# State products in row halves, a fold by transposes, and a new order in phases 0 and 7 of a state-space and butterfly kernel

## What is computed

```python
xz = einsum('bld,ed->ble', layernorm(x), in_proj_w); x_inner, z = split(xz, 2, -1)
x_conv = silu(causal_depthwise_conv(x_inner, conv_w) + conv_b)
x_dbl = einsum('bld,ed->ble', x_conv, x_proj_w)            # 33 wide
delta, B, C = softplus(x_dbl[..., 0]), x_dbl[..., 1:17], x_dbl[..., 17:]
h = h * exp(delta * A) + x_t * delta * B ; y = h @ C        # a scan over tokens
x = x + einsum('bld,od->blo', (y + x_conv * D) * silu(z), out_proj_w)
h = butterfly(layernorm(x) @ W_exp + b_exp, up_weights)     # 10 stages
x = x + butterfly(gelu(h + up_bias), down_weights) @ W_con + b_con + down_bias
```

## Time and profile before

| | |
|---|---|
| median of 3 runs | 568.49 us (566.38 to 570.36) |
| the profiled execution | 569.59 us, of which span 567.9 us |
| TensorE (PE) busy | 528.9 us, 93% of the span |
| VectorE (DVE) busy | 409.6 us, 72% |
| ScalarE (ACT) busy | 306.1 us, 54% |
| GpSimd (POOL) busy | 109.5 us, 19% |
| mean granted TensorE clock | 0.966 of 2.4 GHz |

### The profile page before, as it was taken

The page is one execution under the profiler, slowest core; times in us unless marked ns, Lnnn a source line. Parts: engine busy times, 40 slices in busy tenths (PEclk is TensorE's granted clock), DMA queues, the critical chain, the costliest instruction groups (busy, mean ns, idle before and its releaser), DMA issues.

```text
span 567.9 us, 8152 instructions
## 1 busy us (share of the span) xinstructions
PE 528.9 (93%) x2996; PEld 430.3 (76%) x2996; DVE 409.6 (72%) x860; ACT 306.1 (54%) x526; POOL 109.5 (19%) x96
## 2 busy tenths in 40 slices
PE   3998899888999999999999999999999999699896
PEld 3766676776897779887888778877888788578886
DVE  4859999587983799468966799379946894575532
ACT  2876883865239622874268623962287417431342
POOL 4042100230201301050103120130105021411110
PEclk9986979799999999999999999999999999799999
DMA  8542311200012001210112001200021002100011
GB/s 244 97 27 3 80 35 38 76 2 2 23 52 74 4 2 48 66 39 2 37 41 74 0 9 68 71 8 1 5 73 38 0 2 74 41 1 0 6 34 37
DMA packets 42619, 21.75 MB, mean 38 GB/s; under 512 B 26419, under 2 KB 41011, under 8 KB 42580
## 3 DMA queue, kind: packets, MB, share of 16 engines
q1 hardware_dynamic: 39940, 17.57, 13.0%
q10 hardware_dynamic: 2640, 3.67, 2.3%
HBM read 16.78 MB, written 4.46 MB: 37 GB/s over the span
## 4 chain that ended last, share of the span: by engine, by line
PE 48%; DVE 20%; issue 12%; ACT 9%; SPq 6%; POOL 3%; DMA 0%; DVEq 0%; ACTq 0%; POOLq 0%
PE wide L711 12%; PE acc L844 9%; PE wide L833 7%; SPq L420 5%; PE wide L822 4%; DVE xc L1552 2%; DVE xc L1555 2%; POOL x1b_xn L598 2%; DVE state L1516 2%; DVE hid_low L1429 2%; PE wide L804 2%; PE small L731 2%; PE wide L811 2%; DVE xc L1412 2%; ACT L1054 2%
## 5 line engine op out<-in xcount | busy, mean ns | idle before, releaser
L1054 ACT ACTIVATE hid_f<-wide,bias_up 128x512 f32<-128x512 f32 x64 | 44.0, 687 | 162.0 <-PE wide L833 161.6
L1412 DVE SCALAR_TENSOR_TENSOR xc<-xi,taps,xc 128x512 f32<-128x512 f32 x96 | 87.0, 911 | 4.0 <-ACT xc L1085 1.7
L844 PE MATMUL acc<-w_down_high,hid_high 128*128 128x256 f32 x256 | 73.2, 286 | 5.6 <-DVE hid_low L1429 5.4
L844 PE MATMUL acc<-w_down_high,hid_low 128*128 128x256 f32 x256 | 71.9, 281 | 0.0
L844 PE MATMUL acc<-w_down_low,hid_high 128*128 128x256 f32 x256 | 71.9, 281 | 0.0
L1429 DVE TENSOR_TENSOR hid_low<-hid_f,hid_high 128x512 fp32r<-128x512 f32 x64 | 46.3, 725 | 29.8 <-ACT hid_high L1163 29.2
L833 PE MATMUL wide<-xnT_ln2T_high,w_up_high 128*128 128x512 f32 x128 | 55.4, 432 | 3.4 <-DVE xnT_ln2T_low L1423 1.8
L522 POOL TENSOR_TENSOR rstd<-var_eps,minus_half 128x4 f32<-128x4 f32 x16 | 19.1, 1192 | 202.8 <-DVE var_eps L1317 202.8
L711 PE MATMUL wide<-xnT_ln1T_high,w_in_high 128*128 128x512 f32 x128 | 56.5, 441 | 1.1 <-DVE xnT_ln1T_low L1423 1.0
L822 PE MATMUL wide<-w_out,xc 128*128 128x256 f32 x256 | 56.7, 379 | 0.3 <-DVE xc L1555 0.3
L844 PEld LDWEIGHTS acc<-w_down_high,hid_high 128*128 128x128 f32 x256 | 48.0, 188 | 11.2 <-issue 8.2
(11 more groups left out here) (185 smaller groups left out, 1054.6 us busy)
## 6 DMA issues: line engine op xcount, KB each, us to landing
x_res<-in_L_attn_x_dram SPq DMA_DIRECT2D x9, 512.0 KB, 3.5
c_near<-c_of_tokens SPq DMA_DIRECT2D x8, 512.0 KB
out_dram<-x1b_xn SPq DMA_DIRECT2D x8, 512.0 KB, 2.9
x_ln<-in_L_attn_x_dram SPq DMA_DIRECT2D x7, 512.0 KB, 3.6
xc<-in_L_attn_in_proj_w_dram ACTq DMA_DIRECT2D x2, 512.0 KB, 7.1
xc<-in_L_ffn_W_exp_dram ACTq DMA_DIRECT2D x1, 1024.0 KB, 10.8
x1b_xn<-in_L_ffn_W_con_dram ACTq DMA_DIRECT2D x1, 1024.0 KB, 14.5
raw_out<-n_L_attn_out_proj_w_dram ACTq DMA_DIRECT2D x1, 512.0 KB, 7.0
```

Source lines behind the costliest of these rows:

```text
L844: last = pe.matmul(acc[:, c, :], hid[h][:, j % HRING, c * P:(c + 1) * P], w_down[w][:, j, 0:DM], start=j == 0 and c % 2 == 0 and n == 0, s ...
L1054: ins = act.activation(out_ap, in_ap, how.pop("func"), **how)
L1412: ins = dve.scalar_tensor_tensor(xc[u % BATCH][:, e, :], xi[:, e, tap:tap + TILE], taps[:, e, tap:tap + 1], xc[u % BATCH][:, e, :], ALU.mu ...
```

## The change

1. `ssm_output` is split into two calls, one for each pair of channel blocks, with `up(p, 3)` and `down(p, 1)` between them. The state products use half the rows at a time: the states at the starts of groups 0 and 1 lie in rows 0 to 63 and serve tokens 0 to 255, those of groups 2 and 3 in rows 64 to 127 serve tokens 256 to 511. A bank now holds one half of the tokens of two channel blocks. `gates` follows: four operations of 256 columns and two of 512 for a pair.
2. `xd_tokens_first` transposes all 128 rows and VectorE adds the halves while it reads (`take_xd`); `fold` is gone.
3. VectorE: `convolve(v, 1)` moves ahead of `diagonal_times_c`, `low_hidden(p, 0)` and the low parts of w_down ahead of `assemble`.
4. ScalarE loads the gelu table behind `copy_first_state`.
5. GpSimd: `residual_with_bias(u - 1)` moves to the head of unit u and no longer waits for the gates of u; memsets at the start move ahead of a reciprocal root.
6. Phase 0: the order of input products, light products and low parts. `low_parts(2)` moves ahead of `first_residual(0)`.
7. Phase 7: `up(p, 0)` to `up(p, 2)` move ahead of `step_sums`.
8. `last_ffn`: the last two down products, the last add and the last store go in halves of 256 tokens.

```diff
@@ the bank orders
-    WIDE_ORDER += uses(("up", range(3)), of=phase - 1) + uses(("y", range(CB)), of=phase)
-    WIDE_ORDER += uses(("up", range(3, 5)), of=phase - 1) + uses(("out", range(2)), of=phase)
+    WIDE_ORDER += uses(("up", range(3)), of=phase - 1) + uses(("y", range(2)), of=phase)
+    WIDE_ORDER += uses(("up", [3]), of=phase - 1) + uses(("y", range(2, CB)), of=phase)
+    WIDE_ORDER += uses(("up", [4]), of=phase - 1) + uses(("out", range(2)), of=phase)
@@ SyncE
-            store(UNITS - 1)
+            sp.wait_ge(first_half_final, 1)
+            store(UNITS - 1, slice(0, GR // 2))
+            read(sp, UNITS - 1, "down", 0)
+            store(UNITS - 1, slice(GR // 2, GR))
@@ GpSimd
             for u in range(UNITS):
+                if u:
+                    residual_with_bias(u - 1)
                 weigh_gaps(u)
...
-                if u:
-                    wait(pool, gated, u, CB)
-                    residual_with_bias(u - 1)
                 rstd_of(u, 1, var2, rstd2)
@@ TensorE
-                    last = pe.matmul(bank[:, c * P:c * P + XD], xdT[:, c * P:(c + 1) * P], fold[:, :], start=True, stop=True)
+                    last = pe.transpose(bank[:, c * P:(c + 1) * P], xdT[:, c * P:(c + 1) * P], ident[:, :])
...
+            def ssm_output(u, pair):
+                banks = [tile_of("y", 2 * pair + h, u) for h in range(2)]
+                for h in range(2):
+                    free(pe, u, "y", 2 * pair + h)
...
+                for q in range(2):
+                    g = 2 * pair + q
+                    for c in range(GR):
+                        at = q * HALF_TILE + c % 2 * P
+                        pe.matmul(banks[c // 2][:, at:at + P], x_tok[:, c, g * P:(g + 1) * P],
+                                  m_mat[:, c * P:(c + 1) * P], start=q == 0 and c % 2 == 0, stop=False,
+                                  skip_group_check=True)
...
+                for q in range(2):
+                    g = 2 * pair + q
+                    for h in range(2):
+                        rows = slice(2 * SLOT * h, 2 * SLOT * (h + 1))
+                        last = pe.matmul(banks[h][:, q * HALF_TILE:(q + 1) * HALF_TILE],
+                                         state[u % BATCH][rows, g * P:(g + 1) * P],
+                                         c_startT[rows, h * HALF_TILE:(h + 1) * HALF_TILE],
+                                         start=False, stop=q == 1, skip_group_check=True)
...
+                if v == UNITS:
+                    for j in range(3):
+                        up(p, j)
                 step_sums(u)
...
+                down(u, HB - 2, first)
+                down(u, HB - 1, first).then_inc(first_half_down, 1)
+                down(u, HB - 2, second)
+                down(u, HB - 1, second)
@@ ScalarE
                 copy_first_state(u)
+                load_gelu_table()
                 gelu(p, 0)
@@ VectorE
-                mark_read(dve.tensor_copy(xd[:, :, :], tile_of("xdtok", 0, u)[:, :]
-                                          .rearrange("p (c w) -> p c w", w=P)[:, :, 0:XD]), "xdtok", 0, u)
+                mark_read(dve.tensor_reduce(xd[:, :, :], tile_of("xdtok", 0, u)[:, :]
+                                            .rearrange("p (c h w) -> p c w h", h=2, w=HALF)[:, :, 0:XD, :], AXIS_X, ALU.add), "xdtok", 0, u)
...
+            def gates(u, pair):
+                own = xc[u % BATCH]
...
+                for h in range(2):
+                    written(dve, u, "y", 2 * pair + h)
+                    tokens = slice(h * HALF_TILE, (h + 1) * HALF_TILE)
+                    for q in range(2):
+                        g = 2 * pair + q
+                        ins = dve.scalar_tensor_tensor(own[:, g, tokens], own[:, g, tokens], skip[:, g:g + 1],
+                                                       tile_of("y", 2 * pair + h, u)[:, q * HALF_TILE:(q + 1) * HALF_TILE],
+                                                       ALU.mult, ALU.add)
...
+                for g in (2 * pair, 2 * pair + 1):
+                    dve.tensor_tensor(own[:, g, :], own[:, g, :], z[u % BATCH][:, g, :], ALU.mult).then_inc(gated.handle, 1)
...
                 add_blocks(UP, 0)
                 add_blocks(UP, 1)
+                low_parts(2, "ln1T")
                 first_residual(0, 0)
                 first_residual(0, 1)
                 second_stats(0)
-                low_parts(2, "ln1T")
                 second_normalise(0)
```

## The result

The changed kernel takes 572.1 us in the median of 9 runs (570.8 to 572.9), the kernel before 568.2 in the same comparison: ratio 1.0067, 95% interval 1.0047 to 1.0087. Forecast was 561.7, with a range from 555 to 568, so the forecast was off by 10.4 us, and had the sign wrong too. The profiled execution has a span of 570.2 us at a mean granted clock of 0.961 (before 567.9 at 0.966).

What follows compares the result with a forecast made beforehand. TensorE was taken to bound middle phases, VectorE the end of phase 0, waits phase 7. Gains 6.2 + 1.65 - 2.3 - 0.1 + 1.35 = 6.8 took 569.6 to 562.8; less 1.1 to the median, 561.7 us, range 555 to 568.

Steps and rivals of the forecast that it cites:

- State products: Middle phases, TensorE: row halves work at once and save 0.65 a pair, 1.3 a phase.
- The new wait of 1: Middle phases: TensorE waits about 1 us for the gates ahead of the second y pair, in place of 0.42.
- two diagonal operations, `hid_low` 0.65, assemble: Middle phases, VectorE: part of the sum from `diagonal_times_c` at 22.9 to the gates at 33.3.
- The wait of about 5.5: Phase 7: TensorE waits about 5.5 us before the first up product.
- the later halves: Phase 7: the later halves give 0.7 back.
- the forecast loss: Phase 7: moving the up products ahead of `step_sums` loses 2.3; bounds loss 4 to gain 1.
- VectorE's order gets 1.0 shorter: Phase 0: input products among the light products and early low parts save 1.0; bounds -2 to +1.8.
- eight smaller gates at 0.35: Phase 0, VectorE: eight smaller gates cost 0.35, leaving a gain of 0.65.
- The hold of `second_normalise`: Boundary of phases 0 and 1: GpSimd's x1b add of unit 0 holds `second_normalise` 2.4.
- 1.1 of gain here: Phase 1 wins 1.1 by the mechanism of the steady phases.
- the 1.35: End: the last add and store in halves gain 1.35.
- the one that ends slower: Rival, 7%: row halves run one after the other, each change of shape costs 0.35; total 573.6.

Runs made afterwards that it cites:

- e4: The changed kernel with each state product on all 128 rows of the array instead of 64: 574.8 us.
- e8: e1 with the second convolve block, `convolve(v, 1)`, back behind the gates: 564.6 us.
- e9: e8 with `low_hidden(p, 0)` back behind `assemble`: 558.4 us.
- e1: The changed kernel with phase 7's three up products back behind off_diagonal: 564.4 us.
- e7: e1 with e3's phase 0, tile 2's low parts late, e2's add, `convolve(v, 1)` behind the gates and no early gelu table: 568.9 us.
- e10: e9 with e6's repairs, unit 6's x1b add at its old place, and tile 2's transposes between phase 0's out projections: 558.5 us.
- e11: e10 with the old order of phase 0 on TensorE, ScalarE and VectorE: 555.9 us.
- e3: The changed kernel with `first_phase` of TensorE, ScalarE and VectorE in the old order: 571.4 us.
- e5: The changed kernel with phase 0's gates moved on VectorE ahead of `first_stats(2)` and `first_normalise(2)`: 571.7 us.
- e6: e1 with the repairs of e2 and e5, and tile 2's low parts behind `second_stats`: 561.9 us.
- e12: e11 with `assemble` ahead of the low parts of w_down and of `hid_low`: 554.8 us.
- e2: The changed kernel with GpSimd's x1b add of unit 0 back at its old place, behind all gates: 570.8 us.

## Why the prediction was wrong, step by step

**Middle phases: right in size, wrong in what bound them.** Transposes and reduction: row 0.65 instead of 1.08. State products: 1.72 - 1.06 = 0.66 a pair, as forecast (0.65); against eight instructions on all rows (e4) it is 0.53. The new wait of 1 came (0.96), and one of 0.22 for the states that the sum didn't have. Phase 3 came out at 60.3 against the 60.05 of the forecast. But I laid that wait to the six taps. That the diagonal came late (23.0) was right; it was not what bound, because `hid_low` held the rest at 25.1 to 25.5 anyway (e8). My sum listed "two diagonal operations, `hid_low` 0.65, assemble" as if `hid_low` could start at any time. The gates stood behind the first up product, and undoing that one line gives 1.4 a phase (e9).

**Phase 7: three terms each a little off.** The wait of about 5.5 came (5.78). `step_sums` stands 18.35 into the phase where 17.95 was forecast; that both come out at 496.6 in the trace is luck, since the phase begins 0.4 earlier. The chain to y takes 12.9 instead of 12.3. And the later halves give back 0.3, not 0.7. Together that is the 1.4 by which the forecast loss was too small. What I didn't look at is the other change without this move: there (e1) the chain isn't 17.55 any more but 14.8. Of these 2.7, 1.2 is the early gelu table (e7, without it, takes 16.0), and 1.6 is a clock that rose earlier in these two executions than in the kernel before: from `step_sums` to the first up product it is 9.2 in both, 10.8 before, and 11.3 in e9, which stayed at the lower level. I had credited the move with 5.25 on the chain; it costs the phase 6.4 by these profiles.

**Phase 0: a term with the wrong sign, from VectorE alone.** "VectorE's order gets 1.0 shorter" is the failed step. I counted VectorE's work alone. Phase 0 lost 2.4 where 0.65 was to be gained. By e10 against e11 the new order loses 2.6; its largest new wait is TensorE's 3.4 for `mixed`, on ScalarE, behind a step that the change moved. In the changed kernel as it stands, the old order gave only 0.6 (e3): the second y pair then waits for the first gates. For the new banks the sum had eight smaller gates at 0.35, and no term for that wait (1.12 in the changed kernel, 3.14 in e7, 4.69 in e3, none before).

**The boundary: sized about right.** The hold of `second_normalise` was forecast at 2.4 and is 2.0. TensorE's wait of 2.09 for the low parts went, and it waited 1.65 and 3.21 for the chain of `second_normalise`, softplus and first taps instead; the low parts, moved ahead of the residual, add their 1.29 to that chain. Softplus of unit 1 begins 10.1 into phase 1 instead of 8.6, 1.5 later; the forecast had 1.2 with 0.65 gained ahead of it, so 1.85.

**Phase 1: a clock that fell, and a step not seen.** The forecast had 1.1 of gain here and no term for the clock. Behind the wait of 3.21 the changed kernel ran 10.2 us at the lower level; e1, with the same instructions and the same wait, stayed at the upper one. The sum of phases 0 and 1 is 2.1 less in e1, so about that much of the 6.7 is not the order of these phases, and 4.6 stay. The wait alone doesn't decide it: e3, e5 and e9 have it and fell, e8 has it and didn't; e6 and e10 to e12, where it is 1.4, didn't. What decides is open. `assemble` behind w_down's low parts costs about 0.7 more by the profile of e12, less than one profile can show here; in its rows the states begin 1.4 earlier into the phase.

**The end.** 1.0 of 1.35. The two last adds take 0.69 each, and from the start of the last add to the end it is 3.3 instead of 4.6: the 1.35 came. The 0.4 that lack lie ahead of the last add (45.0 from the out projection, 44.7 before).

**What stays open.** The single repairs e2, e3 and e5 gave 1.3, 0.6 and 0.4, less than their waits; e6 and e10 say the same. I take it that a wait which goes uncovers the next, and that the clock moves with them, but that is not shown. Of the 6.6 that were missed in phases 0 and 1, only the order of phase 0 was separated by runs (2.6, and that in e10's surroundings); the 2.1 of the clock rest on two profiles of the same instructions. What e7 keeps of the change and loses 4.3 by in these phases, the banks in token halves above all, was never put back there alone. e12 still has 146.2 in phases 0 and 1 against 144.9 before.

Of the rivals none came. The nearest was the one that ends slower, but not by its mechanism: the row halves run at once (e4).

## What to carry to other kernels

When an operation is moved up an in-order queue, ask first what it waits for, and count everything behind it from then on: one low part ahead of `assemble` cost 1.4 us a phase, more than the 1.05 us of TensorE's time that the row halves saved. A wait that disappears is worth only the distance to the next one, so follow the chain behind it to its last engine before booking a gain. Two edits on the same chain don't add: price each with the other already in (the old order of phase 0 gave 0.6 with the gates late, 2.6 with the gates first). And where two kernels with the same instructions in a stage differ by 2 us, as here in phases 0 and 1, a smaller difference there can't be read as an edit's from one profile.

## What the runs showed of the hardware

- Two products on 64 rows each run at once on the array: eight instructions of 256 columns in 1.13 us, against 1.97 and 1.89 on 128 rows (e4), and 1.05 us of TensorE's busy time less a phase.
- GpSimd's operation of 1024 numbers also holds a VectorE operation that reads one tile and per-partition scalars: `second_normalise` 3.41 instead of 1.38. The rows before showed it for two tiles. The Trainium skill (SBUF — State Buffer, SBUF: two separate sides) says the same of VectorE operations with two SBUF inputs or in a two-port mode; the trace agrees, and doesn't show which of the two holds here.
- Same instructions, other clock: phase 0 was granted 0.92 in one execution and 0.53 in another over the same 16 us, and took 74.2 and 77.0. The clock there isn't all: the changed kernel was at the lower level from 41.5 to 58.5 too, and took 72.1; from 82 us on it was granted 0.97 and 1.00 where e8 had 0.64 and 0.83. In one kernel (e2) the mean clock went from 0.955 to 0.976 over ten executions, and the time from 572.8 to 566.9. By the Trainium skill (TensorE: Matmul & The Clock Gate, Part 1) the window over which the gate watches TensorE runs free and isn't reset when a kernel starts; levels that differ for the same instructions fit that, and don't prove it.
- A switch of ScalarE's table set took 1.28 us with ScalarE busy right up to it, and the next activation started 0.02 us after it (rows at 260.85 and 262.15 of the changed kernel).
